# Two-layer macaron block on one core: low halves later, projection inside the heads' tail, result stored by tiles, 20 unread products ahead of each norm's transposes

## What is computed

```python
x = x + 0.5 * L0_ffn(layernorm(x))    # dense 512x512, a rank-32 adapter mixed by soft routing over 8 experts
x = x + L0_attn(layernorm(x))         # 32 heads of 16, rotary, causal, plus a 10-token prefix; projection by w_proj
x = x + 0.5 * L0_ffn(layernorm(x))
x = x + 0.5 * L1_ffn(layernorm(x))    # 16 experts of width 128, the best 2 per token, and a shared expert of 512
x = x + L1_attn(layernorm(x))         # 32 query heads of 128, 8 key/value heads, not causal; projection by wo
x = x + 0.5 * L1_ffn(layernorm(x))
```

## Time and profile before

| what | us |
|---|---|
| three timed runs, median | 1753.16 (1752.48 to 1755.58) |
| the profiled execution, own time | 1739.47 |
| its span, first to last instruction | 1737.7 |
| TensorE busy | 1595.8 (92%), mean granted clock 0.972 |
| VectorE busy | 992.1 (57%) |
| ScalarE busy | 911.1 (52%) |
| GpSimd busy | 984.9 (57%) |
| transfers | 180.21 MB, mean 104 GB/s |

### The profile page before, as it was taken

How to read it: one execution, slowest core, us unless ns; L and a number is a source line. 1 busy time by engine, 2 the same in 40 slices (tenths; PEclk the granted TensorE clock), 3 DMA queues, 4 the chain that set the end, 5 groups by cost and what they waited for, 6 DMA issues and landing times. The chain is left out here.

```text
span 1737.7 us, 26665 instructions
## 1 busy us (share of the span) xinstructions
PE 1595.8 (92%) x8364; PEld 1249.9 (72%) x8364; DVE 992.1 (57%) x2614; ACT 911.1 (52%) x1881; POOL 984.9 (57%) x1156
## 2 busy tenths in 40 slices
PE   6799999997889996889999999999999999979997
PEld 4587566556577885678788777787777788767885
DVE  6742665644583246566656656565666656666235
ACT  2212777751132223777777667676776767731231
POOL 2443555630314632788877778777787777812543
PEclk9999999998999998999999999999999999989999
DMA  2200000001076643544353453534445344444935
GB/s 88 104 1 3 2 2 2 1 1 38 1 270 235 227 146 103 109 109 116 83 119 97 104 126 97 115 85 105 110 106 121 73 106 88 89 172 162 348 127 157
DMA packets 311210, 180.21 MB, mean 104 GB/s; under 512 B 281495, under 2 KB 282855, under 8 KB 308656
## 3 DMA queue, kind: packets, MB, share of 16 engines
q1 hardware_dynamic: 299248, 152.54, 32.0%
q0 software_dynamic: 11840, 26.25, 4.8%
HBM read 111.08 MB, written 22.54 MB: 77 GB/s over the span
## 5 line engine op out<-in xcount | busy, mean ns | idle before, releaser
L1375 POOL TENSOR_TENSOR st_prob<-st_prob,st_rinv 128x512 f32<-128x512 f32 x256 | 269.9, 1054 | 186.8 <-DVE st_rinv L1443 186.8
L1379 POOL TENSOR_TENSOR st_plane<-st_prob,st_plane 128x512 f16<-128x512 f32 x256 | 307.7, 1212 | 0.1
L1294 ACT ACTIVATE st_plane<-st_prob 128x512 f16<-128x512 f32 x256 | 160.9, 629 | 116.7 <-POOL st_prob L1375 116.5
L1310 ACT ACTIVATE st_prob<-st_score,st_nmax 128x512 f32<-128x512 f32 x256 | 175.1, 684 | 63.9 <-DVE st_nmax L1450 61.3
L1450 DVE TENSOR_REDUCE st_nmax<-st_score 128x1 f32<-128x512 f32 x256 | 175.0, 684 | 42.4 <-PE st_score L114 39.5
L1289 ACT ACTIVATE st_pthi<-st_plane_t 128x512 fp32r<-128x512 f16 x256 | 159.5, 623 | 18.5 <-issue 13.8
L1420 DVE CAST st_ptlo<-st_plane_t 128x512 fp32r<-128x512 f16 x256 | 157.5, 616 | 1.7 <-DMA st_plane_t<-st_plane 1.7
L2092 DVE CUSTOM_DVE_ANT_0 st1b_dump<-st1b_score,st1b_maskrow 128x128 f32<-128x128 f32 (+3 forms) x256 | 112.8, 488 | 78.0 <-PE st1b_score L1779 53.0
L1424 DVE TENSOR_TENSOR st_olo<-st_outp,st_ohi 128x512 fp32r<-128x512 f32 x64 | 44.3, 691 | 181.5 <-ACT st_ohi L1298 181.5
L112 PE MATMUL st_outp<-st_pthi,st_vhi 128*128 128x512 f32 x256 | 106.8, 417 | 35.5 <-ACT st_pthi L1289 27.4
L785 POOL DMA_INDIRECT st_xg<-rows,st_source x62 | 62.8, 1012 | 108.0 <-DVE st_source L973 61.4
(11 more groups left out here) (381 smaller groups left out, 4041.4 us busy)
## 6 DMA issues: line engine op xcount, KB each, us to landing
st_raw<-in_moe_w SPq DMA_DIRECT2D x40, 768.0 KB, 7.5
sorted_outs<-st_ln_xn SPq DMA_DIRECT2D x62, 256.0 KB, 3.5
st_qraw<-in_gqa_q SPq DMA_DIRECT2D x8, 1024.0 KB, 5.2
st_oraw<-in_gqa_o SPq DMA_DIRECT2D x8, 1024.0 KB, 5.1
rows<-st_ln_xn SPq DMA_DIRECT2D x2, 2048.0 KB, 14.5
st_kvraw<-in_gqa_kv SPq DMA_DIRECT2D x8, 512.0 KB, 4.1
st_plane_t<-st_plane SPq DMA_TRANSPOSE x256, 2.8
st1a_raw<-in_w_attn SPq DMA_DIRECT2D x3, 1024.0 KB, 5.5
```

Source lines behind the costliest of these rows:

```text
L1294: act.activation(plane[t][:, 0:T], prob[:, t, :], ACT.Copy).then_inc(upper_ready, 1)
L1310: act.activation(prob[:, t, :], score[t][:, :], ACT.Exp, bias=nmax[:, slot:slot + 1], accum_out=rsum[:, slot:slot + 1]).then_inc(exp_ready, 1)
L1375: pool.tensor_tensor(prob[:, t, :], prob[:, t, :], rinv[:, slot:slot + 1].broadcast_to([P, T]), ALU.mult).then_inc(norm_ready, 1)
L1379: pool.tensor_tensor(plane[t][:, T:2 * T], prob[:, t, :], plane[t][:, 0:T], ALU.subtract).then_inc(lower_ready, 1)
```

## The change

Four edits, in the functions named.

1. `gqa_stage`, VectorE: `out_lo`, `k_lo` and `v_lo` move from the end of turn u to the middle of turn u + 1, behind the copy and the factor at t = 1; the second output-weight split of turn 5 moves from t = 0 to t = 1.
2. `heads_block`: the projection's products move into turns 16 and 17, its additions and statistics with them; `projection_block` is gone, with its meeting of the engines. The products of tiles 0 to 3 (batch 0) stand between the last short operations, the first three quarters of tiles 4 to 7 behind `final`, their last quarter at the end.
3. `moe_stage`, last one: SyncE stores each tile of x by itself (eight DMAs of 256 KB), when its last addition is done; `store_stage` is gone.
4. `Norm.tensor`: 20 products of the identity with itself into the last bank, which nobody reads, ahead of the wait for the rows. `warm` (L117) is already used in `heads_block`.

```diff
     def tensor(self, pe):
+        warm(pe, self.bank[-1], self.ident, 20)
         for n, (h, k) in enumerate(self.order):
...
+                if last_stage:
+                    for t in range(NT):
+                        wait(sp, combined, 2 * t + 2)
+                        wait(sp, step_added, kinds.count(False) - NT + 1 + t)
+                        sp.dma_start(env["out"][t * P:(t + 1) * P, :], x[:, t, :]).then_inc(out_stored, 16)
+                    wait(sp, out_stored, 16 * NT)
...
+                def late(g, u):
+                    if u >= 1:
+                        out_lo(g, u - 1)
+                    elif not opening(g):
+                        out_lo(g - 1, NU - 1)
+                    if u == 1:
+                        k_lo(2 * g + 2, 1)
+                    if u == 3:
+                        v_lo(2 * g + 2, 1)
+                    if u == 5 and not final(g):
+                        k_lo(2 * g + 3, 0)
+                    if u == 7 and not final(g):
+                        v_lo(2 * g + 3, 0)
...
                             if t >= 1:
                                 lifted(g, u, t - 1)
-                            if u == 5 and t == 0:
+                            if u == 5 and t == 1:
                                 odd_split_lo(g, 3)
+                            if t == 1:
+                                if u >= 1:
+                                    late(g, u - 1)
+                                elif not opening(g):
+                                    late(g - 1, NU - 1)
...
-                        if u >= 1:
-                            out_lo(g, u - 1)
-                        elif not opening(g):
-                            out_lo(g - 1, NU - 1)
-                        if u == 1:
-                            k_lo(2 * g + 2, 1)
-                        if u == 3:
-                            v_lo(2 * g + 2, 1)
-                        if u == 5 and not final(g):
-                            k_lo(2 * g + 3, 0)
-                        if u == 7 and not final(g):
-                            v_lo(2 * g + 3, 0)
...
                 peeled(dve, KV1, body)
+                late(LAST, NU - 1)
                 add(KV1, 0)
...
+        proj_bank = [score[0], score[1], across[0], across[1], across[2], prep, score[0], score[1]]
...
+                def project(t, first, end):
+                    tok = slice(t * P, (t + 1) * P)
+                    if first == 0:
+                        wait(pe, (maxed, maxed, exp_ready, exp_ready, exp_ready, shift_copied, added, added)[t],
+                             (16 * NU, 16 * NU, 12 * NU, 12 * NU, 12 * NU, 2 * NU, 1, 2)[t])
+                    wait(pe, ohi_ready, GROUPS if end == KC and t >= TB else GROUPS - 1)
+                    wait(pe, olo_ready, GROUPS if end == KC and t >= TB else GROUPS - 1)
+                    for k in range(first, end):
+                        last = three_passes(pe, proj_bank[t][:, :], xhi[:, k, tok], xlo[:, k, tok], wp["hi"][:, k, :], wp["lo"][:, k, :],
+                                            k == 0, k == KC - 1)
+                    if end == KC:
+                        last.then_inc(projected, 1)
+
+                def closing(u):
+                    if u.unit() == NU:
+                        project(0, 0, KC)
+                        values(u, -1, 2)
+                        project(1, 0, KC)
+                        values(u, -1, 3)
+                        adapter_turn(u)
+                        project(2, 0, KC)
+                        tokens(u)
+                        project(3, 0, KC)
+                    else:
+                        final(u)
+                        for t in range(TB, NT):
+                            project(t, 0, KC - 1)
+                        for t in range(TB, NT):
+                            project(t, KC - 1, KC)
...
+                def add(t):
+                    wait(dve, projected, t + 1)
+                    dve.tensor_tensor(x[:, t, :], proj_bank[t][:, :], x[:, t, :], ALU.add).then_inc(added, 1)
...
+                            if u.unit() == NU:
+                                add(0)
+                                add(1)
                             if u.has(-1):
                                 norm(u)
+                            if u.unit() == NU:
+                                add(2)
+                                add(3)
...
+                wait(dve, added, TB)
+                for t in range(TB):
+                    moments.take(dve, t)
+                for t in range(TB, NT):
+                    add(t)
+                    if t > TB:
+                        wait(dve, added, t)
                         moments.take(dve, t - 1)
```

More of the change, by code:

```diff
@@ L525, in moe_stage @@
         y_copied, xg_cleared = s.sem("y_copied"), s.sem("xg_cleared")
-        y_stored = [s.sem(f"y_stored{n}") for n in range(3)]
+        y_stored, out_stored = [s.sem(f"y_stored{n}") for n in range(3)], s.sem("out_stored")
         gathered = [s.sem(f"gathered{n}") for n in range(YG)]
@@ L1860, in final @@
                     last.then_inc(out_ready, 1)
+                def project(t, first, end):
[26 more added lines that the diff above has]
+                            project(t, KC - 1, KC)
                 def turn(u):
+                    if u.unit() >= NU:
+                        closing(u)
+                        return
                     for two in range(6):
@@ L1989, in _ @@
                 pipeline(turn)
+                moments.root_table(act)
             @block.gpsimd
@@ L2153, in _ @@
                 pipeline(turn)
-def projection_block(nc, env, name, wp):
-    x, xhi, xlo = env["x"], env["xhi"], env["xlo"]
-    with ExitStack() as ctx:
-        s = Stage(nc, ctx, name)
-        whi, wlo = wp["hi"], wp["lo"]
-        bank = [s.ps(f"bank{n}", [P, C]) for n in range(4)]
-        out_ready, added = s.sem("out_ready"), s.sem("added")
-        moments = Moments(s, env)
-        with nc.Block() as block:
-            @block.tensor
-            def _(pe):
-                for t in range(NT):
-                    if t >= 4:
-                        pe.wait_ge(added, t - 3)
-                    tok = slice(t * P, (t + 1) * P)
-                    for k in range(KC):
-                        last = three_passes(pe, bank[t % 4][:, :], xhi[:, k, tok], xlo[:, k, tok], whi[:, k, :], wlo[:, k, :],
-                                            k == 0, k == KC - 1)
-                    last.then_inc(out_ready, 1)
-            @block.scalar
-            def _(act):
-                moments.root_table(act)
-            @block.vector
-            def _(dve):
-                for t in range(NT):
-                    dve.wait_ge(out_ready, t + 1)
-                    dve.tensor_tensor(x[:, t, :], bank[t % 4][:, :], x[:, t, :], ALU.add).then_inc(added, 1)
-                    if t >= 1:
-                        dve.wait_ge(added, t)
+                wait(dve, added, TB)
[5 more added lines that the diff above has]
+                        wait(dve, added, t)
                         moments.take(dve, t - 1)
-                dve.wait_ge(added, NT)
+                wait(dve, added, NT)
                 moments.take(dve, NT - 1)
                 moments.close(dve)
-def store_stage(nc, env, out):
-    with ExitStack() as ctx:
-        s = Stage(nc, ctx, "store")
-        stored = s.sem("stored")
-        with nc.Block() as block:
-            @block.sync
-            def _(sp):
-                sp.dma_start(out.rearrange("(t p) c -> p t c", p=P), env["x"][:, :, :]).then_inc(stored, 16)
-                sp.wait_ge(stored, 16)
 def macaron_kernel(nc, dram, out, stages=None):
@@ L2212, in macaron_kernel @@
                "xhi": s.sb("xhi", [P, KC, NT * P], F32R), "xlo": s.sb("xlo", [P, KC, NT * P], F32R)}
+        env["out"] = out
         env["xd"] = nc.dram_tensor("rows", (NT * P, C), F32, kind="Internal").ap()
@@ L2219, in macaron_kernel @@
                 Stage.recycle(nc)
-        store_stage(nc, env, out)
 def constants():
```

10 lines of the change are left out of this document (6 added, 4 removed).

## The result

| | before | after |
|---|---|---|
| timed runs, median | 1754.37 (1752.48 to 1759.10, 4 runs) | 1734.55 (1729.57 to 1739.49, 4 runs) |
| ratio, 95% interval | | 0.9883 (0.9847 to 0.9919) |
| span of the profiled execution | 1737.7 | 1731.1 |
| TensorE busy, mean granted clock | 1595.8, 0.972 | 1624.7, 0.980 |
| VectorE, ScalarE, GpSimd busy | 992.1, 911.1, 984.9 | 998.7, 912.8, 988.7 |

What follows compares the result with a forecast made beforehand. TensorE was taken as the bound, busy 819 of 871 us in grouped-query attention. Terms 5.5 + 3.8 + 1.95 + 5.4 = 16.7 us, taken off the median 1753.16, gave 1736.5 us, range 1722 to 1748.

Steps and rivals of the forecast that it cites:

- ScalarE's idle head of loop not being there: Grouped-query attention: sign that would make the prediction wrong; it assumed ScalarE stands still 2.90 us at its loop's head.
- new stop in turn 0: Grouped-query attention, groups 2 to 6: TensorE stops 1.8 us ahead of the output projection, a loss of 1.1 us each.
- Projection in the tail: Heads' tail: projection products fill TensorE's pauses; TensorE wins 6.6 us, VectorE is late, 5.5 us left, bounds 4 and 7.
- Or the clock shows through: Heads' tail: reason given for the lower bound of 4 us, one copy or the clock showing through.
- Store: End of the kernel: only the last 256 KB store counts, at 3.5 us; gain 3.8 us, between 3 and 5.
- Unread products: Norms: twenty products ahead of the transposes make these run faster; sum +1.95 us, from -3 to +3.5.
- Twenty unread ones at 0.21 take 4.3 us, to 1545.3: they fit: Last expert stage's norm: the products end before TensorE gets its rows at 1545.57; 1.35 us gained there.
- Low halves later: Grouped-query attention: VectorE takes maxima 0 and 1 earlier, shortening TensorE's stops; 5.4 us, bounds 0 and -5.
- No new stop, but no room: Turns 2, 4 and 6: second low half done at +4.7 to +5.2 us, before +5.45, so TensorE doesn't stop.
- Rival 4: Grouped-query attention: ScalarE's 2.90 us go away as code moves, turns 0 lose nothing; 5.5 us more, 1731 us; chance 0.10.
- Rival 1: Grouped-query attention: turn 5's stop shrinks to about 2.1 us and the clock stays up; 12.6 us more, 1724 us; chance 0.12.

Runs made afterwards that it cites:

- experiment 3: Changed kernel without the 20 unread products: 1724.51 us, ratio 0.9894 to the kernel before; changed kernel run again beside it: 1725.11 us, 0.9895.
- Experiment 2: Kernel before with only the projection in the heads' tail and the result stored by tiles: 1723.79 us, ratio 0.9888.
- experiment 1: Kernel before with only the low halves and turn 5's split moved later in grouped-query attention: 1747.38 us, ratio 1.0004.
- experiment 5: Kernel before with tail projection and store by tiles, plus split moved: 1720.04 us; plus split and turn 5's low half: 1714.16; plus all low halves, split unmoved: 1718.21.

## Why the prediction was right, and where not

The total was right (1736.5 for 1734.55, a gain of 16.7 us for 19.8), and that is luck in good part: more than half of the gain comes from something that the sum put at nothing, and its second-largest term is zero. Of the four terms the tail's was right, the store's too small, that of the unread products has no gain behind it, and that of the low halves is zero. The time forecast for the profiled execution, 1722.8 us, was 10 us off (1732.79). The prediction also named what would make it wrong, ScalarE's idle head of loop not being there. It wasn't there in the changed kernel, nor was the new stop in turn 0 that hangs on it.

**Projection in the tail, 5.5 us.** Measured 4.5 from the last unit's values to the next norm (36.5 to 32.0). The mechanism is as forecast: no pause on TensorE, then VectorE late. The sum put VectorE's end 29.7 us after the start of the values, at 417.6; it took 30.8 (391.68 to 422.43). The 1.1 us arise at the head of the tail and not on VectorE, whose first addition of the last four is already late by as much: the values and the first product took 2.0 us, 0.9 in the sum, since the clock was at its lower level there. Where it wasn't, the stretch took 31.0 us and the gain against 36.5 is the 5.5 of the forecast; the kernel before varies too, 35.8 to 36.5. "Or the clock shows through" stood among the bounds.

**Store, 3.8 us.** Measured 5.4 (7.87 to 2.45; in the ten executions that have it 2.45 to 3.32, so 4.5 to 5.4). The term was mis-sized by the price: I took 3.5 us for 256 KB from the stores of sorted outputs, which carry other traffic beside them. From the addition's end the last store took 2.45 us, with only the tail of the other tiles' stores beside it. The Trainium skill, DMA: Bandwidth & Descriptors, "Anatomy of one DMA", gives 2.6 for it by its 2.0 us plus bytes at 436 GB/s, and this case agrees with it, though that page gives it for GpSimd and here SyncE issues it.

**Unread products, +1.95 us.** No gain: 0.6 us between the medians the other way, which is within the noise. The step that failed is "Twenty unread ones at 0.21 take 4.3 us, to 1545.3: they fit": 0.21 us is one record at the lower clock, each product is two, and twenty take 6.2 to 6.9 us, though the clock rises among them. They end 2.2 us after the rows are ready, and what the faster transposes win is paid for there. In stage 2, where I charged 0.3, they stand on the path for all that ScalarE's late start doesn't hide: 2.7 us. What they do to stage 4 is open (experiment 3).

**Low halves later, 5.4 us.** With ScalarE's stop, as the sum assumed it, the term is zero: the interval of the ratio allows a gain of 2.4 us at most. Turn by turn the sum was good in part: the 0.80 us of turn 1 went, turn 0 got its stop (forecast 1.8 us, measured 1.38 to 1.95), and turn 5's came to 1.54 us (forecast 2.1). The step that failed is "No new stop, but no room" for turns 2, 4 and 6: turn 4 stops 0.87 us. The sum had the second low half done at +4.7 to +5.2; in turn 4 it ends at +6.5 (1155.22 to 1161.74), behind the copy that GpSimd's work stretches to 2.67 us. And the fall of the clock, which both sides of the sum left in place, stayed there in this kernel.

**Rival 4** (ScalarE's stop vanishes) is what happened; it had a chance of 0.10 and a price of 5.5 us, for I let it cancel only the new stop of turn 0. Its price against the kernel before is 11.9 us by the ratio of timed runs, 13.9 between the medians (6.6 to 12.1 by stage 4, 865.0 and 870.5 in the two executions of before against 858.4 with the stop away): the two old stops of 1.56 us a group in five groups, and falls of the clock with them. It came through the projection: with that block and its meeting gone ScalarE's list is two recorded instructions shorter ahead of the loop (739 for 741), and the code is no longer loaded anew in each pass.

**Rival 1** (the clock stays up in turn 5) came true as well, not for its reason. It rested on a bound between stops of 1.44 and 2.76 us. Experiment 2 has stops of 2.76 us with the clock at 1.00 behind them, experiment 1 one of 1.54 us with 0.50. The length of the stop alone doesn't decide it.

By these parts edits 2 and 3 give 12 us from ScalarE's stop and the falls that went with it, 5.4 from the store and 4.5 from the tail, 22 in all; alone they gave 20.6 between the medians (19.5 by the ratio). On the same chip edit 1 on top of them costs 0.7 us and edit 4 another 0.6, which leaves the 19.2 of the whole change there. Neither step is clear of noise. By the groups (the table of experiment 5) the edits in grouped-query attention cost 0.8 us in each of six, some 5, and the unread products 2.7 in stage 2. The whole change gave 19.8, 19.2 and 16.8 us between the medians of the three comparisons (20.5, 18.3 and 13.8 by the ratios), so the parts are known to some 3 us and not better.

Carrying the gain over to the median came out right by luck at both ends: the first profile of before had a quick heads' stage (361.5 for 367.5 to 370.2 in the three other executions of that code), and the first profile of after a slow last stage.

## What to carry to other kernels

A gain in a stage that an edit touches need not come from that edit: make each part alone before crediting it, above all where a program with loops has become shorter or longer. Look for a pause "<-issue" at the head of an engine's loop, and for loads of instructions that come with it once a pass; if both are there, try a few idle instructions ahead of the loop before rebuilding the order of the work. And a wait of 181 us on an engine that isn't the bottleneck is no reserve: only the bottleneck's 35 us were, and moving work away from one of its stops brought it another one turn earlier.

## What the hardware showed unexpectedly

- ScalarE's pause at the head of a loop depends on where the loop lies in its list: 2.3 to 2.9 us at one place, none two recorded instructions earlier or sixty later, 1.8 to 2.0 four later. With the pause the trace has five loads of instructions a pass on q14, without it none. One pass is 279 recorded instructions. The Trainium skill, Runtime: NRT & Kernel Launch, "Instruction fetch mechanics", says that most engines hold 512 instructions, in two blocks of 256, and TensorE 2048, and that a taken branch whose target isn't held waits for a fetch. That fits: by an estimate from these figures 279 lie in two blocks but for 22 starting places of 256, and TensorE with 971 records a pass never paused at its loop's head. The loads here come in pieces of 8 KB on q14 and 16 KB on q8 (0.58 MB in 71 and 0.84 in 51); how much an engine holds no run here shows.
- Removing the pause won 1.56 us of TensorE's stops a group and, in most groups, a fall of the clock worth 1.2 to 1.7 us, though the longest stop, 2.76 us, stayed as it was. What decides about the fall stays open.
- An fp32 product of 128x128 by 128x128 that isn't a transpose is two records, each 0.21 us from start to start at the lower clock and 0.11 at the upper; a transpose of the same size is one, 0.11 us at the upper (3.66 us for 32).
- VectorE's low copy of a transposed tile took 2.65 to 2.68 us beside GpSimd's 2.4 us low half of the weights, in all 36 groups of the six executions with later low halves, and 0.4 us where GpSimd stood still.
